# An eight-chunk tail of a recurrence moved from three steps of a software pipeline into eight

## The chip, the cores and the metric

The kernel runs on one core of one Trainium2 chip. The metric is the time of one execution on the device in microseconds. A core has a matrix engine (TensorE, PE in the profile), a vector engine (VectorE, DVE), a scalar engine (ScalarE, ACT), GpSimd (POOL) and a queue that issues transfers (SyncE, SP). Each engine runs its own instructions strictly in the order in which they are written, and the engines wait for each other by semaphores. PE's clock is granted at one of two levels, 1.2 or 2.4 GHz; the profile gives it as a share of the higher.

## What is computed

An input x of 2048 tokens by 128 features goes through two residual blocks. The first is a linear layer trained while it runs: a scan over all tokens, each of which changes the matrix W. The second is six layers of windowed attention and a gated feed-forward part over the same tokens.

```python
def step(W, inp):
    xt, vt = inp
    y = xt @ W.T
    err = y - vt
    gW = scale * (err.T @ xt)
    return (W - eta * gW, y)
_, ys = jax.lax.scan(step, W0, (xs, vs))
...
for i in range(DEPTH):
    x = attn_layer(shift_tokens(x), Wqkv[i], q_scale[i], k_scale[i], Wo[i]) + x
    x = ffn_layer(shift_tokens(x), ln_g[i], ln_b[i], W1[i], b1[i], W2[i], b2[i]) + x
...
x = x + _layernorm(_L0_attn_ref(_layernorm(x, axis=-1), ...), axis=-1)
x = x + _layernorm(_L0_ffn_ref(_layernorm(x, axis=-1), ...), axis=-1)
```

## The kernel before

**Tiles and chunks.** The 2048 tokens are 16 tiles of 128. For the scan the same 128 tokens are called a chunk. The part of the scan inside each chunk is solved for all chunks ahead of time (up to about 57 us). What is left is a chain over the chunks, since W passes from one to the next. Chunk c takes four instructions, each of which waits for the one before: PE's `chain_w` (L436, a product with W), VectorE's `chain_u` (L745, subtracts), PE's `chain_d` (L444, the update's product) and VectorE's `chain_W` (L751, adds it to W, `wT`). `chain_w` of the next chunk needs the new W.

**Units.** The results of the chunks go on in groups, `UNITS` = tiles (0,1), (2,3), (4 to 7), (8 to 11), (12 to 15). For unit u: `result(u)` on VectorE (an addition L760 with two inputs in SBUF, statistics L764 and L769); `layer_norm(u, 0)` on GpSimd (four small instructions, L1283 to L1289), then on ScalarE (L1023); `total(u)` on VectorE (the residual, L777 to L785); `layer_norm(u, 1)` on GpSimd and ScalarE; `features(u)` on PE (L453, a transpose into a bank of PSUM) and `featured(u)` on ScalarE (L1032, L1033), which fills x0S, the input of the main stage. Tile t can be projected when its unit's features are there.

**The main stage.** It begins at about 77 us and is a software pipeline written out by hand: every engine runs a loop over s, and in turn s it does the first part of tile s, the second of tile s-1 and so on down to tile s-5 (96 pairs of layer and tile, then the feed-forward parts in groups of four tiles). Per tile, PE projects keys and queries into psq (L257), in two halves of 16 products; VectorE reads each half twice (L947 and L961 for the first, L825 and L841 for the second) before ScalarE squares it (L1124, L1200), and only then may PE write the next half. GpSimd adds and scales (L1332, L1391, L1352, L1368), PE transposes the result into two of four ring banks (L267), scores it (L298), and VectorE takes the maximum (L983), subtracts (L816), sums (L857), GpSimd normalises (L1373), VectorE transposes (L978) and PE mixes (L309) with the values (L279). VectorE's L947 for tile t waits for the projection of tile t and for the transposes of tile t-2. The ring of four PSUM banks is handed out in the order of PE's program by `take`; a product waits until its bank's former contents are copied out. The chain and the features take banks from the same ring.

**Where the chain sits.** Chunks 0 to 3 and units 0 and 1's results run ahead of the loop. The others have slots inside the turns: `chunk_at(s, j)` says which chunk has slot j of turn s, and `unit_at(s, lag)` which unit has a slot in turn s. Slots 0 and 1 are in turn s (slot 0 before L947 of tile s, slot 1 after it), slots 2 and 3 stand in turn s+1. In GpSimd's loop `layer_norm(u, 0)` stands between L1352 and L1368, and `layer_norm(u, 1)` ahead of L1346. SP loads the second layer's projection matrix into `wqk[:, 1]`, which holds `c_xn`, an operand of `chain_d`, until the last chunk is through.

Of the kernel before, what the change touches and what calls it, by code (L numbers as in the profile page):

```python
# [16 lines left out]
QUAD = 4  # L17
GROUPS = TILES // QUAD
# [19 lines left out]
UNITS = [(0, 2), (2, 2), (4, 4), (8, 4), (12, 4)]  # L38
# [9 lines left out]
def group_at(s, lag):  # L48

    n = s - lag  # L50
    return n // QUAD if n >= 0 and n % QUAD == 0 and n // QUAD < ALLG else -1


def chunk_at(s, j):

    return QUAD * (s + 1) + j if 0 <= s < GROUPS - 1 else -1


def unit_at(s, lag):

    u = s - lag + 2
    return u if 1 <= u < len(UNITS) else -1


def build(nc, x_d, wvT_d, w0T_d, bv_d, eta_d, wqk_d, scale_d, mvT_d, wo_d, w1_d, w2_d, par_d,
          ident_d, rep_d, mask_d, rope_d, kfac_d, level_d, out_d):
    ctx = ExitStack()
    with ctx:
# [157 lines left out]
        def wait(eng, s, value):  # L226

            if isinstance(value, int) and value <= 0:
                return
            eng.wait_ge(s, value)  # L230
# [15 lines left out]
        def _(pe):  # L246
# [261 lines left out]
            for s in range(STEPS + 20):  # L508
                if chunk_at(s - 1, 1) >= 0:
                    chain_w(chunk_at(s - 1, 1))  # L510
# [15 lines left out]
                if chunk_at(s - 1, 1) >= 0:  # L526
                    chain_d(chunk_at(s - 1, 1))
# [49 lines left out]
                if chunk_at(s - 1, 3) >= 0:  # L577
                    chain_w(chunk_at(s - 1, 3))
                u = unit_at(s, 3)
                if u >= 0:  # L580
                    features(u)
# [100 lines left out]
        def _(dve):  # L682
# [123 lines left out]

            for s in range(STEPS + 20):
                u = unit_at(s, 2)
                if u >= 0:
                    total(u)  # L810
# [89 lines left out]
                if i >= 0:  # L900
# [5 lines left out]
                    v.scalar_tensor_tensor(uT[0:rows, 2, :], ring[bank][0:rows, :], par[0:rows, i // GROUPS, 4:5],  # L906
                                           uT[0:rows, 2, :], ALU.add, ALU.mult).then_inc(freed[bank], 1)
                u = unit_at(s, 1)
                if u >= 2:
                    result(u)  # L910
# [483 lines left out]
        @block.sync  # L1394
        def _(sp):
            x_v = x_d.rearrange("(t p) d -> p t d", p=P)

            def load_x(g):
                sp.dma_start(xmid[:, QUAD * g:QUAD * g + QUAD, :], x_v[:, QUAD * g:QUAD * g + QUAD, :]).then_inc(a_x[g], 16)

            load_x(0)
            sp.dma_start(ident[:, :], ident_d).then_inc(s_ident, 16)
            load_x(1)
            sp.dma_start(eta_bc[:, :], eta_d.partition_broadcast(P)).then_inc(s_level, 16)
            load_x(2)
            sp.dma_start(level, level_d).then_inc(s_level, 16)
            load_x(3)
            for dst, src in ((wvT, wvT_d), (wT[:, :], w0T_d), (bv, bv_d.partition_broadcast(P))):
                sp.dma_start(dst, src).then_inc(s_const, 16)
            for dst, src in ((kfac[:, :], kfac_d), (mask_in, mask_d), (rope[:, :, :], rope_d), (rep_in, rep_d),  # L1410
                             (qk_scales[:, :, :], scale_d.partition_broadcast(P)), (par[:, :, :], par_d)):
                sp.dma_start(dst, src).then_inc(s_tables, 16)
            sp.dma_start(wqk[:, 0, :], wqk_d[0]).then_inc(wqk_ready, 16)

            def load_m(l):
                sp.dma_start(mvT[:, :, :], mvT_d[l]).then_inc(mw_ready, 16)
                sp.dma_start(wo[:, :, :], wo_d[l].rearrange("(a p) n -> p a n", p=P)).then_inc(mw_ready, 16)

            def load_w1(l):
                sp.dma_start(w1[:, :], w1_d[l]).then_inc(w1_ready, 16)  # L1420

            def load_w2(l):
                sp.dma_start(w2[:, 0:2, :], w2_d[l, 0:256, :].rearrange("(a p) n -> p a n", p=P)).then_inc(w2_ready, 16)
                sp.dma_start(w2[0:HID + 1 - 256, 2, :], w2_d[l, 256:HID + 1, :]).then_inc(w2_ready, 16)

            load_m(0)
            load_w1(0)
            load_w2(0)
            bank, n = place["H3", 0]
            sp.wait_ge(filled[bank], n + 1)  # L1430
            load_m(1)
            out_v = out_d.rearrange("(t p) d -> p t d", p=P)

            for s in range(STEPS + 20):
                i = group_at(s, 8)
                if i >= 0:
                    g = i % GROUPS
                    bank, n = place["Y", QUAD * i + QUAD - 1]
                    sp.wait_ge(freed[bank], n + 1)
                    wait(sp, xh_ready, i)  # L1440
                    tiles = slice(1 + QUAD * g, 1 + QUAD * g + QUAD)
                    sp.dma_start(xf[:, 0], x1[:, 0, tiles, :]).then_inc(xf_ready, 16)
                    sp.dma_start(xf[1:P, 1], x1[0:P - 1, 1, tiles, :]).then_inc(xf_ready, 16)
                    sp.dma_start(xf[0:1, 1], x1[P - 1:P, 1, QUAD * g:QUAD * g + QUAD, :]).then_inc(xf_ready, 16)
                l = s // TILES
                if s == GROUPS:
                    bank, n = place["cd", TILES - 1]
                    sp.wait_ge(filled[bank], n + 1)
                    sp.dma_start(wqk[:, 1, :], wqk_d[1]).then_inc(wqk_ready, 16)
                if s % TILES == 0 and 1 <= l < LAYERS - 1:  # L1450
                    sp.wait_ge(pq_done, TILES * l)
                    sp.dma_start(wqk[:, (l + 1) % 2, :], wqk_d[l + 1]).then_inc(wqk_ready, 16)
                if s % TILES == LOAD_M and l < LAYERS - 2:
                    bank, n = place["H3", l + 1]
                    sp.wait_ge(filled[bank], n + 1)
                    load_m(l + 2)
                if s % TILES == LOAD_W and 1 <= l < LAYERS:
                    bank, n = place["A2", GROUPS * l - 1]
                    sp.wait_ge(filled[bank], n + 1)
                    load_w1(l)  # L1460
                    bank, n = place["Z", GROUPS * l - 1]
                    sp.wait_ge(filled[bank], n + 1)
                    load_w2(l)
                i = group_at(s, 18)
                if i >= LASTG:
                    g = i - LASTG
                    sp.wait_ge(f_out, g + 1)
                    sp.dma_start(out_v[:, QUAD * g:QUAD * g + QUAD, :], xmid[:, QUAD * g:QUAD * g + QUAD, :]).then_inc(s_out, 16)

            sp.wait_ge(s_out, 16 * GROUPS)  # L1470
# [81 lines left out]
```

## Time and profile before

| | us |
|---|---|
| median of 3 runs | 1506.65 (1505.9 to 1509.11) |
| profiled execution | 1507.59 |
| its span, first to last instruction | 1505.8 |
| PE busy | 1441.7 |
| VectorE busy | 1327.1 |
| GpSimd busy | 1209.8 |
| ScalarE busy | 1162.2 |

The span is cut below into steps: a step runs from VectorE's start of L947 for one tile to its start for the next. Step 0 begins at 81.6 us. In the rows of the timeline the columns are start, length (both us), engine, line, operation, output and input, count, and in brackets the idle time just before it and what ended it.

### The profile page before, as it was taken

To read this page: it belongs to the slowest core of one execution; us is meant where nothing else is said; L and a number is where in the kernel's file an instruction comes from. 1 tells how busy PE (TensorE), PEld (TensorE's weight loads), DVE (VectorE), ACT (ScalarE), POOL (GpSimd) and SP (SyncE) were. 2 spreads that over 40 slices of the span, in tenths; PEclk is the share of its full clock that TensorE was granted. 3 is DMA by queue.
4 is the path that set the end of the run, shared out by engine and by line. 5 is a ranking of instruction groups with operands and counts; after the bars stand their busy time and mean duration, and the time that the engine had idled before them with its cause. 6 is when DMAs were issued, how large, how long until landed. Compare 5 with 4: busy or idle time off the path is not lost.

```text
span 1505.8 us, 74802 instructions
## 1 busy us (share of the span) xinstructions
PE 1441.7 (96%) x32904; PEld 785.9 (52%) x32904; DVE 1327.1 (88%) x1789; ACT 1162.2 (77%) x2289; POOL 1209.8 (80%) x1051
## 2 busy tenths in 40 slices
PE   6877999999999999999999999999999999999985
PEld 6823444545545545545545545545555545545553
DVE  5478999989999989999999999989999999999974
ACT  4337888878888788888888888888888788888871
POOL 5148999878888888888888888888888888888841
PEclk9968999999999999999999999999999999999998
DMA  5100000020000020000020000020000000000000
GB/s 206 30 1 30 3 10 10 3 66 10 4 20 15 4 66 10 3 20 15 3 66 10 4 19 15 4 66 10 3 20 15 4 10 10 4 20 15 4 17 29
DMA packets 24564, 32.93 MB, mean 22 GB/s; under 512 B 2372, under 2 KB 21424, under 8 KB 23344
## 3 DMA queue, kind: packets, MB, share of 16 engines
q1 hardware_dynamic: 24240, 28.15, 5.8%
q8 instruction: 260, 4.26, 1.2%
q14 instruction: 64, 0.52, 0.1%
HBM read 20.80 MB, written 1.05 MB: 15 GB/s over the span
## 4 chain that ended last, share of the span: by engine, by line
PE 89%; DVE 5%; issue 2%; POOL 2%; ACT 1%; DMA 1%; SPq 0%; POOLq 0%; DVEq 0%; ACTq 0%
PE psq L257 22%; PE ring L279 21%; PE ring L309 11%; PE pss L298 9%; PE ring L267 9%; PE ring L323 8%; PE ring L333 4%; PE ring L346 1%; DVE qa L825 1%; PE ring L382 1%; DVE qb L841 1%; DVE mx L983 1%; DVE qb L961 1%; DMA xf<-x 0%; DMA mh<-in_bv 0%
## 5 line engine op out<-in xcount | busy, mean ns | idle before, releaser
L279 PE MATMUL ring<-mh,x0S 128*32 128x512 f32 x3072 | 407.9, 595 | 0.0
L257 PE MATMUL psq<-wqk,x0S 128*32 128x512 f32 x3072 | 394.9, 612 | 5.9 <-ACT sq L1200 4.9
L1332 POOL TENSOR_TENSOR qa<-qa,qb 128x1024 f32<-128x1024 f32 x96 | 229.2, 2388 | 6.7 <-DVE qb L961 6.7
L1391 POOL TENSOR_TENSOR qa<-qa,qb 128x1024 f32<-128x1024 f32 x96 | 228.6, 2382 | 0.0
L309 PEld LDWEIGHTS ring<-u,pT 128*32 128x32 f32 x6144 | 171.4, 111 | 61.8 <-issue 60.1
L309 PE MATMUL ring<-u,pT 128*32 128x128 f32 x6144 | 191.6, 274 | 4.1 <-DVE pT L978 4.1
L1373 POOL TENSOR_TENSOR pr<-pr,rden 128x1024 f32<-128x1024 f32 x96 | 183.9, 1916 | 12.8 <-DVE rden L860 12.8
L257 PEld LDWEIGHTS psq<-wqk,x0S 128*32 128x32 f32 x3072 | 93.6, 111 | 184.2 <-issue 168.4
L1352 POOL TENSOR_TENSOR qa<-qa,rn 128x1024 f32<-128x1024 f32 x96 | 182.7, 1903 | 0.2
L1368 POOL TENSOR_TENSOR qa<-qa,rn 128x1024 f32<-128x1024 f32 x96 | 182.8, 1904 | 0.0
L298 PEld LDWEIGHTS pss<-kT,qT 64*32 64x32 f32 x12288 | 134.8, 105 | 91.1 <-issue 83.6
L947 DVE TENSOR_TENSOR qa<-psq,tab 128x1024 f32<-128x1024 f32 x96 | 117.5, 1224 | 71.3 <-PE ring L267 71.0
L298 PE MATMUL pss<-kT,qT 64*32 64x64 f32 x12288 | 166.6, 224 | 2.6 <-issue 2.4
L279 PEld LDWEIGHTS ring<-mh,x0S 128*32 128x32 f32 x3072 | 95.5, 109 | 134.0 <-issue 120.8
L267 PEld LDWEIGHTS ring<-ident,qa 64*128 64x128 f32 x3072 | 111.5, 139 | 78.1 <-issue 50.7
L1346 POOL TENSOR_TENSOR tab<-rope,qk_scales 128x256 f32<-128x256 f32 x96 | 70.6, 736 | 101.2 <-DVE qb L841 101.2
L323 PE MATMUL ring<-xh,w 128*32 128x512 f32 (+1 forms) x1056 | 148.2, 594 | 1.2 <-ACT xh L1170 1.2
L1200 ACT ACTIVATE sq<-psq 128x1024 f32<-128x1024 f32 x96 | 98.2, 1023 | 60.0 <-DVE qb L841 58.6
L267 PE MATMUL ring<-ident,qa 64*128 64x64 f32 x3072 | 136.6, 229 | 5.2 <-issue 3.0
L825 DVE TENSOR_TENSOR qa<-psq,tab 128x1024 f32<-128x1024 f32 x96 | 116.9, 1218 | 9.4 <-PE psq L257 8.5
L983 DVE TENSOR_REDUCE mx<-pss 128x16 f32<-128x1024 f32 x96 | 114.8, 1196 | 10.4 <-PE pss L298 10.4
L978 DVE STREAM_TRANSPOSE pT<-pr 128x1024 f32<-128x1024 f32 x96 | 118.7, 1237 | 2.9 <-POOL pr L1373 2.7
(172 smaller groups left out, 2724.3 us busy)
## 6 DMA issues: line engine op xcount, KB each, us to landing
wqk<-in_wqk SPq DMA_DIRECT2D x6, 1024.0 KB, 8.6
mvT<-in_mvT SPq DMA_DIRECT2D x6, 512.0 KB, 3.8
wo<-in_wo SPq DMA_DIRECT2D x6, 512.0 KB, 5.2
xf<-x SPq DMA_DIRECT2D x24, 128.0 KB
xf<-x SPq DMA_DIRECT2D x24, 127.0 KB
rope<-in_rope SPq DMA_DIRECT2D x1, 2048.0 KB, 10.0
w<-in_w SPq DMA_DIRECT2D x6, 341.0 KB, 3.0
xmid<-in_x SPq DMA_DIRECT2D x4, 256.0 KB, 4.2
```

The costliest lines, as they stand in the source:

```text
L257: last = mm(psq[WIN * w:WIN * w + WIN, 512 * (n % 2):512 * (n % 2) + 512], x0S[:, tile * P + WIN * w:tile * P + WIN * w + WIN], wqk[:, l % ...
L267: last = tr(banks[r][:, 64 * blk:64 * blk + 64], src(blk)[rows], ident[rows, rows])
L279: last = mm(bank[WIN * g:WIN * g + WIN, :], x0S[:, tile * P + WIN * w:tile * P + WIN * w + WIN], mh[:, l % 2, g, :, :].rearrange("p j n -> ...
L298: last = mm(pss[WIN * g:WIN * g + WIN, col:col + KEYS], qT[rows, pair, WIN * w:WIN * w + WIN], kT[rows, t % 2, pair, WIN * w:WIN * w + KEY ...
L309: last = mm(bank[WIN * w:WIN * w + WIN, 0:P], pT[:, half, b * P + WIN * w:b * P + WIN * w + WIN], u4[:, slot, v_w, b * P:b * P + P], start ...
L323: last = mm(bank[c:c + m, :], w1[:, col + c:col + c + m], xnT[:, :], start=True, stop=True)
L825: v.tensor_tensor(a3[t % 2][:, 0:16, :], q3, tab[:, t % 2, 0, :].unsqueeze(1).broadcast_to([P, HEADS, HD]), ALU.mult)
L1332: g_.tensor_tensor(qa[:, t % 2, 1024:2048], qa[:, t % 2, 1024:2048], qb[:, 1024:2048], ALU.add).then_inc(sum_k, 1)
L1352: g_.tensor_tensor(a3[t % 2][:, 16:32, :], a3[t % 2][:, 16:32, :], rn[:, 16:32].unsqueeze(2).broadcast_to([P, HEADS, HD]), ALU.mult).then_ ...
L1368: g_.tensor_tensor(a3[t % 2][:, 0:16, :], a3[t % 2][:, 0:16, :], rn[:, 0:16].unsqueeze(2).broadcast_to([P, HEADS, HD]), ALU.mult).then_inc ...
L1373: g_.tensor_tensor(p4[t % 2], p4[t % 2], rden[:, :].unsqueeze(1).unsqueeze(3).broadcast_to([P, 2, HEADS, WIN]), ALU.mult).then_inc(p_ready, 1)
L1391: g_.tensor_tensor(qa[:, t % 2, 0:1024], qa[:, t % 2, 0:1024], qb[:, 0:1024], ALU.add).then_inc(sum_q, 1)
```

## The change

In three steps of the loop four chunks each are replaced by a table. Chunks 4 to 7 and unit 1 and 2 keep their slots. Chunk 8 moves from slot 0 of turn 1 to slot 1 of turn 1; chunks 9 to 15 have slot 0 of turns 2 to 8, one each. Unit 3's slots move from those of s - lag = 1 to s - lag = 4, and unit 4's from 2 to 8. The load of the second layer's projection matrix moves from turn 4 to turn 8, since it must follow chunk 15.

```diff
--- before.py
+++ after.py
@@ -51,15 +51,19 @@
     return n // QUAD if n >= 0 and n % QUAD == 0 and n // QUAD < ALLG else -1
 
 
+CHUNKS = {(0, 0): 4, (0, 1): 5, (0, 2): 6, (0, 3): 7, (1, 1): 8, (2, 0): 9, (3, 0): 10, (4, 0): 11,
+          (5, 0): 12, (6, 0): 13, (7, 0): 14, (8, 0): 15}
+UNIT_STEP = {-1: 1, 0: 2, 4: 3, 8: 4}
+
+
 def chunk_at(s, j):
 
-    return QUAD * (s + 1) + j if 0 <= s < GROUPS - 1 else -1
+    return CHUNKS.get((s, j), -1)
 
 
 def unit_at(s, lag):
 
-    u = s - lag + 2
-    return u if 1 <= u < len(UNITS) else -1
+    return UNIT_STEP.get(s - lag, -1)
@@ -1443,7 +1447,7 @@
                 l = s // TILES
-                if s == GROUPS:
+                if s == 2 * GROUPS:
                     bank, n = place["cd", TILES - 1]
                     sp.wait_ge(filled[bank], n + 1)
                     sp.dma_start(wqk[:, 1, :], wqk_d[1]).then_inc(wqk_ready, 16)
```

Counted in steps as cut above, the chunks whose four instructions fall into each are, before: 5 to 8 in step 0, 9 to 12 in step 1, 13 to 15 in step 2; after: 5 to 7, then 8 and 9, and one in each of steps 2 to 7 (10 to 15). On VectorE result(3) moves from step 1 to step 4, total(3) from 2 to 5, result(4) from 2 to 8, total(4) from 3 to 9.

## Rows read from the trace of the kernel before

**Rows 1.** Page, part 1: busy us, share of span, instructions.

```profile
PE 1441.7 (96%) x32904; PEld 785.9 (52%) x32904; DVE 1327.1 (88%) x1789; ACT 1162.2 (77%) x2289; POOL 1209.8 (80%) x1051
```

**Rows 2.** Steps 0 to 11: stretch, length, busy by engine, PEclk, DMA share, GB/s.

```profile
81.60:98.00 16.40, 11.54 (x48) 4.39 (x48) 13.88 (x29) 4.20 (x8) 7.49 (x11) 0.69 0.00 1
98.00:115.40 17.40, 12.92 (x68) 5.42 (x68) 13.74 (x34) 6.23 (x17) 10.94 (x16) 0.71 0.00 0
115.40:130.60 15.20, 12.39 (x172) 5.69 (x175) 13.20 (x32) 11.08 (x27) 11.20 (x14) 0.89 0.20 70
130.60:146.60 16.00, 11.23 (x189) 4.14 (x190) 13.96 (x22) 12.19 (x26) 15.51 (x17) 0.89 0.01 3
146.60:159.40 12.80, 12.51 (x317) 6.51 (x295) 12.10 (x14) 11.12 (x24) 10.71 (x10) 1.00 0.01 3
159.40:171.50 12.10, 11.97 (x319) 6.08 (x296) 12.00 (x14) 9.61 (x20) 10.97 (x10) 1.00 0.01 3
171.50:183.90 12.40, 12.19 (x316) 6.13 (x294) 12.10 (x14) 9.69 (x20) 11.73 (x10) 1.00 0.02 5
183.90:196.80 12.90, 12.90 (x323) 6.96 (x308) 12.06 (x13) 10.50 (x22) 12.22 (x10) 1.00 0.06 16
196.80:209.60 12.80, 12.65 (x356) 6.66 (x343) 12.69 (x17) 10.26 (x21) 11.77 (x10) 1.00 0.04 11
209.60:222.40 12.80, 11.58 (x256) 5.61 (x257) 12.27 (x19) 9.69 (x21) 12.48 (x14) 1.00 0.01 3
222.40:235.00 12.60, 12.00 (x320) 6.11 (x298) 12.14 (x14) 10.37 (x22) 11.91 (x10) 1.00 0.01 3
235.00:247.40 12.40, 12.40 (x316) 6.30 (x298) 12.05 (x13) 10.48 (x22) 11.71 (x10) 1.00 0.06 17
```

**Rows 3.** Timeline of VectorE: the end of step 0, chunks 8 and 9.

```profile
97.75 0.35 DVE L751 SCALAR_TENSOR_TENSOR wT<-ring,coef,wT 128x128 f32<-128x128 f32 x1 [1.86 <-PE ring L444]
98.02 1.22 DVE L947 TENSOR_TENSOR qa<-psq,tab 128x1024 f32<-128x1024 f32 x1
99.15 0.28 DVE L745 TENSOR_TENSOR x0S<-ring,x0S 128x128 f32<-128x128 f32 x1
```

**Rows 4.** Timeline of PE: projections in steps 0, 3 and 6.

```profile
93.34 3.64 PE L257 MATMUL psq<-wqk,x0S 128*32 128x512 f32 x16
...
142.21 3.54 PE L257 MATMUL psq<-wqk,x0S 128*32 128x512 f32 x16 [3.64 <-ACT sq L1200]
...
181.13 1.92 PE L257 MATMUL psq<-wqk,x0S 128*32 128x512 f32 x16
```

**Rows 5.** Page, part 5: busy us, mean ns of one, idle time before.

```profile
L1200 ACT ACTIVATE sq<-psq 128x1024 f32<-128x1024 f32 x96 | 98.2, 1023 | 60.0 <-DVE qb L841 58.6
```

**Rows 6.** Timeline of VectorE: result(2) with its successor, total(4) with its successor.

```profile
92.58 0.69 DVE L760 TENSOR_TENSOR x0T<-x0T,x0S 128x512 f32<-128x512 f32 x1
...
94.50 0.26 DVE L745 TENSOR_TENSOR x0S<-ring,x0S 128x128 f32<-128x128 f32 x1
...
134.11 2.20 DVE L777 TENSOR_TENSOR xmid<-xmid,x0T 128x512 f32<-128x512 f32 x1
...
137.55 1.19 DVE L816 TENSOR_TENSOR pr<-pss,mx 128x1024 f32<-128x1024 f32 x1
```

**Rows 7.** Timeline of GpSimd around layer_norm(4, 0).

```profile
125.79 1.91 POOL L1352 TENSOR_TENSOR qa<-qa,rn 128x1024 f32<-128x1024 f32 x1
129.65 0.20 POOL L1283 TENSOR_TENSOR lvare<-lmv,eps 128x4 f32<-128x4 f32 x1 [1.95 <-DVE lmv L769]
...
131.52 1.90 POOL L1368 TENSOR_TENSOR qa<-qa,rn 128x1024 f32<-128x1024 f32 x1
```

**Rows 8.** Timeline of VectorE: L978 in step 6.

```profile
174.14 1.25 DVE L978 STREAM_TRANSPOSE pT<-pr 128x1024 f32<-128x1024 f32 x1 [0.19 <-POOL pr L1373]
```

**Rows 9.** Timeline of PE: the transposes at the end of step 4.

```profile
158.51 0.71 PE L267 MATMUL ring<-ident,qa 64*128 64x64 f32 x16 [0.29 <-ACT x0S L1033]
```

**Rows 10.** Timeline of PE: a stall in the second layer.

```profile
309.33 0.97 PE L298 MATMUL pss<-kT,qT 64*32 64x64 f32 x48 [2.37 <-issue]
```

## The prediction, made before the changed kernel was run

> **What bounds the kernel now.** I read the table of engine shares first, then the main stage's opening cut into steps, then single rows of the timeline. Over the whole span PE is busy 96%, and a reader could stop there [rows 1]. The change touches only the first twelve steps of the main stage, and there the table by step says something else [rows 2]. I cut it where VectorE starts L947 for the next tile, so that one row is one step and a delay anywhere ends up in some row's length. Steps 0 to 3 last 16.4, 17.4, 15.2 and 16.0 us at a mean granted clock of 0.69 to 0.89, and no engine is full: this is latency. From step 4 a step takes 12.1 to 12.9 us, and in it VectorE is busy 12.0 to 12.7, PE 11.6 to 12.9 and GpSimd 10.7 to 12.5. So the change moves work from steps in which engines wait for each other into steps in which three engines are nearly full. After step 11 PE is full and later steps only carry the shift on. The question is thus what L947 of tile 12 (now at 247.4) does.
>
> **What the first steps give back.** Up to chunk 7 nothing moves. In step 0 VectorE waits 1.86 us for chunk 8's second product before it can start L947 [rows 3]; in the new order chunk 8 comes after L947, so tile 1 starts at about 95.8, just after the projection that began at 92.1 instead of 93.3 [rows 4]. That is -2.2 us. What then limits a step is the loop through psq: project, two VectorE passes, a square of 1.02 [rows 5], and the same again. A projection costs 3.64 at the low clock and 1.92 at the high one [rows 4]. Step 1 has two at the low clock: 2 x 3.6 + 4 x 1.2 + 2 x 1.0, and 2.7 for the features of tiles 2 and 3, chunk 9 and the transpose that the loop also passes, is 16.7. Step 1 loses result(3) and two of its four chunks, step 2 loses total(3), result(4) and two of three chunks, step 3 loses total(4) and gets chunk 11; I walked steps 2 and 3 in the same way as step 1. Step 2 has its second projection at the high clock, because PE then works without a gap for some six microseconds: 13.4. In step 3, total(4) no longer keeps VectorE from releasing psq (it holds it from 134.11 to 137.55 [rows 6]), PE's idle 3.64 before a 3.54 projection [rows 4] shrinks to about 1.1, and the projection costs 1.92: 12.0. Steps 0 to 3 become 14.2, 16.7, 13.4 and 12.0 against 16.4, 17.4, 15.2 and 16.0: **-8.7**. If PE stays at the low clock in both disputed projections the gain is 3.3 less, -5.4; if it were high in all the others too, three more projections give 1.65 each, -13.7.
>
> **What the later steps pay.** Four things arrive in steps 4 to 9. (a) One chunk a step in 4 to 7. On VectorE L745 and L751 have 0.28 and 0.35 [rows 3], of which overlap leaves about 0.2 and 0.27 (97.75 to 98.02): 0.47 a step in a step that has 0.1 to 0.8 idle. On PE a chunk adds two products, some 0.85; that binds only in step 7, where PE is busy 12.90 of 12.90 and VectorE has room [rows 2]. (b) result(u) in steps 4 and 8: 92.58 to 94.50, 1.92, if GpSimd leaves it alone; total(u) in steps 5 and 9 costs about 2.0 likewise, but 3.44 where its first instruction met a running GpSimd one, 2.20 instead of 0.69 [rows 6]. (c) GpSimd's layer_norm(u, 0) stands in its queue ahead of L1368 and L1373. Now it waits 1.95 for result(4)'s statistics, and L1368 starts at 131.52, 3.8 after L1352 ended at 127.70 [rows 7]. There nobody needed GpSimd. In a full step VectorE's L978 has already waited 0.19 for L1373 [rows 8], so a delay of 3.8, less what result(u) itself adds on VectorE, goes through to L978: about 1.8. (d) While VectorE does all this PE has nothing: I get gaps of 3.5 and 5.7 us before the projections for tiles 6 and 10, like the 3.64 that preceded a low-clock projection, so 1.65 more each.
>
> Step 4: 12.12 of VectorE work + 0.47 + 1.92 = 14.5 (from 12.8, **+1.7**). PE's second product of chunk 12 waits there for a chain_u that is queued behind result(3), some 1.6 us, and the transposes of tile 3 behind it; they end as VectorE gets there, so this costs nothing beyond the 14.5. Step 5: 12.1 + 0.47 + 2.0 + 1.8 + 1.9 (projection and chain at the low clock) = 18.3 (from 12.1, **+6.2**). Step 6: 12.1 + 0.47 + 0.7 for featured(3), which frees a ring bank that the transpose wants (a wait for it of 0.29 stands in step 4 now [rows 9]) = 13.3 (from 12.4, **+0.9**). Step 7: 12.9 + 0.85 = 13.8 (**+0.9**). Step 8: 12.8 + 1.92 = 14.7 (**+1.9**). Step 9: 12.8 + 2.0 for L978 + 3.55 for total(4), which meets L1391 here because GpSimd has the feed-forward part's first statistics in that step too (12.48 of 12.80 [rows 2]), + 1.6 for the clock, less 0.4 of idle = 19.6 (**+6.8**). Step 10: +0.3 for featured(4). Together **+18.7**.
>
> The 1 MB load of wqk[1] moves on SP from step 4 to step 8, behind the xf loads. Tile 16 needs it eight steps, some 100 us, later: nothing waits for it.
>
> **Sum.** -8.7 + 18.7 = +10.0. The profiled execution took 1507.59 (span 1505.8), the median is 1506.65, 0.9 lower; on the median this gives 1516.6, and I say **1516.5**, slower by 0.66%.
>
> A rule of the Trainium skill stands beside (b): the page GPSIMD Engine Reference, section Specifications, says that GpSimd shares its SBUF interfaces with VectorE and that the conflict is with VectorE instructions that have two SBUF inputs. The 2.20 against 0.69 is what that looks like. I take the long form for one of the four moved instructions; by the rule alone, with GpSimd busy nearly all the time, all four would pay it, about 4 us more.
>
> **The rivals.** *Hidden in the slack.* VectorE is idle 0.1 to 0.8 in each of steps 4 to 11, 3.4 in all [rows 2]. The moved VectorE work is 4 x 0.47 + 2 x 1.92 + 2 x 2.0 = 9.7. If GpSimd's queue and the clock cost nothing, the later steps pay between 9.7 - 3.4 = 6.3 and 9.7, and the whole is -2.4 to +1.0: 1504 to 1508. For it: GpSimd too is idle 0.3 to 2.1 in each of these rows. Against it: L978 already waits for L1373. The Trainium skill, Perfetto Trace Analysis, section Optimization Strategy, says that interleaving regimes with different bounds may help; by it the time would come out at this rival's.
>
> *Faster.* With VectorE and PE no longer waiting for the chain, the clock rises in step 1 rather than step 2, and all projections of steps 1 and 2 cost 1.92. The gain is then 13.7, and if the later steps pay only the 9.7 less 3.4 the time is 1506.65 - 7.4 = 1499. It decides if PE's gaps ahead of those projections nearly vanish; I count 2 to 3 us in each, since both VectorE passes and the square lie between two projections, so it is unlikely.
>
> *A late clock.* PE has fewer products in steps 2 and 3 than now, and the clock stays low to tile 4: gain 5.4, time 1520.
>
> *The load in a worse place.* PE once stood 2.37 us with no releaser [rows 10] right as SP issued xf loads and a wqk load. The new step 8 puts these two together: +2.4 if it recurs, 1519. Now only one of the later loads shows as much.
>
> *Nothing moves*, because the chain's waits are replaced one for one by others: covered by the first rival's 1507.
>
> **How the numbers follow.** Forecast 0.50; hidden in the slack 0.18, of which 0.03 below 1503.6; faster 0.07; late clock 0.15; the load 0.10. The measurement can tell about 0.2%, 3 us, from no change. So faster 0.10, same 0.15, slower 0.75. The range takes in the two slower rivals and half of the slack rival: 1505 to 1520.5. It leaves out the faster case and all collisions at once.
>
> **What would show it.** L947 by tile, shift against now: -2.2, -2.9, -4.7, -8.7 for tiles 1 to 4, then -7.0, -0.8, 0, +1, +3, +10, +10 up to tile 11. L978 waiting 1.5 to 2 us for L1373 in steps 5 and 9; GpSimd waiting about 2 us or more for L769 twice among full steps; 3.5 us projections for tiles 6 and 10. I am wrong if tile 4 is not at least 5 us earlier, or if steps 5 and 9 stay under 15 us.

## The result, and the profile of the changed kernel

| | before | changed |
|---|---|---|
| median of 5 runs each | 1505.9 | 1518.14 |
| lowest to highest | 1501.76 to 1509.11 | 1515.67 to 1520.56 |
| profiled execution, its span | 1507.59, 1505.8 | 1518.14, 1516.1 |

The ratio is 1.0085, 95% interval 1.0061 to 1.011: the change makes the kernel slower by 0.85%. The changed kernel was timed once more, beside the last experiments, with 1.0058 (1.004 to 1.0075). The time is in the forecast range; the forecast point was 1516.5.

In the listings of the changed kernel every line from the loops on has a number 4 higher: L951 is the L947 of before, L982 the L978, L261 the L257. The first view is the page's part 1, which answers to [rows 1].

```profile
PE 1443.2 (95%) x32904; PEld 786.7 (52%) x32904; DVE 1326.0 (87%) x1789; ACT 1162.1 (77%) x2289; POOL 1210.3 (80%) x1051
```

Nothing is to be seen there: the same instructions, all engines busy as long as before to 1.5 us, and the span 10.3 us longer. The next view cuts the same stretch as [rows 2] at VectorE's starts of L951, one row for each of steps 0 to 11 (stretch, length, busy by engine, PEclk, DMA share, GB/s).

```profile
81.60:96.30 14.70, 11.39 (x45) 3.88 (x45) 13.37 (x27) 2.81 (x4) 5.39 (x8) 0.58 0.00 1
96.30:112.60 16.30, 10.91 (x65) 4.05 (x67) 10.08 (x20) 7.58 (x20) 14.04 (x16) 0.65 0.00 0
112.60:126.50 13.90, 10.87 (x96) 3.86 (x100) 7.73 (x9) 7.68 (x18) 7.59 (x8) 0.75 0.01 2
126.50:138.70 12.20, 10.50 (x260) 4.97 (x245) 11.34 (x14) 8.90 (x19) 9.91 (x9) 1.00 0.01 1
138.70:153.60 14.90, 12.97 (x313) 6.67 (x298) 14.41 (x24) 9.60 (x20) 11.30 (x12) 1.00 0.02 4
153.60:169.90 16.30, 12.89 (x321) 6.69 (x308) 14.44 (x25) 11.89 (x26) 15.69 (x16) 1.00 0.01 2
169.90:183.40 13.50, 13.50 (x329) 7.07 (x308) 12.70 (x17) 11.42 (x24) 12.67 (x11) 1.00 0.01 2
183.40:198.80 15.40, 14.12 (x336) 7.73 (x313) 12.76 (x16) 10.75 (x22) 13.43 (x11) 1.00 0.07 20
198.80:213.40 14.60, 14.43 (x376) 7.11 (x360) 14.46 (x26) 11.06 (x22) 8.38 (x9) 1.00 0.23 77
213.40:233.50 20.10, 13.32 (x226) 5.83 (x231) 15.85 (x27) 12.23 (x28) 19.37 (x22) 0.76 0.01 2
233.50:246.50 13.00, 12.79 (x324) 6.80 (x309) 12.24 (x14) 11.00 (x24) 10.34 (x10) 0.98 0.01 3
246.50:258.80 12.30, 12.30 (x327) 6.43 (x305) 11.99 (x14) 10.51 (x22) 11.19 (x10) 1.00 0.06 17
```

Steps 0 to 3 are 7.8 us shorter than before, steps 4 to 11 are 19.2 longer, and steps 5 and 9 hold 11.5 of that. Their sum is +11.4 while the span is 10.3 longer, so 1.1 us is given back after step 11; what lies there is told of below the table of steps. What ended the waits in the two long steps is in the timeline. The next rows are VectorE's, in steps 5, 7 and 9; the last of them begins step 10.

```profile
157.88 1.25 DVE L982 STREAM_TRANSPOSE pT<-pr 128x1024 f32<-128x1024 f32 x1 [1.75 <-POOL pr L1377]
160.16 0.80 DVE L781 TENSOR_TENSOR xmid<-xmid,x0T 128x512 f32<-128x512 f32 x1
197.99 0.35 DVE L755 SCALAR_TENSOR_TENSOR wT<-ring,coef,wT 128x128 f32<-128x128 f32 x1 [2.10 <-PE ring L448]
218.15 1.25 DVE L982 STREAM_TRANSPOSE pT<-pr 128x1024 f32<-128x1024 f32 x1 [2.00 <-POOL pr L1377]
220.43 2.43 DVE L781 TENSOR_TENSOR xmid<-xmid,x0T 128x512 f32<-128x512 f32 x1
233.52 1.22 DVE L951 TENSOR_TENSOR qa<-psq,tab 128x1024 f32<-128x1024 f32 x1 [2.16 <-PE ring L271]
```

The two L982 rows answer to [rows 8], where the wait was 0.19: VectorE now waits 1.75 and 2.00 us for GpSimd's normalisation L1377. Why that is late is in GpSimd's rows, which answer to [rows 7].

```profile
152.19 0.20 POOL L1287 TENSOR_TENSOR lvare<-lmv,eps 128x4 f32<-128x4 f32 x1 [1.95 <-DVE lmv L773]
154.07 1.90 POOL L1372 TENSOR_TENSOR qa<-qa,rn 128x1024 f32<-128x1024 f32 x1
...
212.47 0.20 POOL L1287 TENSOR_TENSOR lvare<-lmv,eps 128x4 f32<-128x4 f32 x1 [2.71 <-DVE lmv L773]
214.34 1.90 POOL L1372 TENSOR_TENSOR qa<-qa,rn 128x1024 f32<-128x1024 f32 x1
```

GpSimd stands 1.95 and 2.71 us in layer_norm(u, 0), waiting for result(u)'s statistics, and the tile's own work (L1372, L1377) waits in its queue behind it. PE's projections, which answer to [rows 4], complete the picture.

```profile
123.36 1.92 PE L261 MATMUL psq<-wqk,x0S 128*32 128x512 f32 x16
...
166.76 1.92 PE L261 MATMUL psq<-wqk,x0S 128*32 128x512 f32 x16 [2.54 <-ACT sq L1204]
...
194.51 1.16 PE L350 MATMUL ring<-wo,mvT 64*128 64x128 f32 x16 [1.17 <-ACT u L1217]
...
217.13 3.56 PE L261 MATMUL psq<-wqk,x0S 128*32 128x512 f32 x16
...
228.66 3.64 PE L261 MATMUL psq<-wqk,x0S 128*32 128x512 f32 x16 [4.50 <-ACT sq L1204]
```

In step 9 PE is idle 4.50 us and then projects at the low clock, 3.64 us instead of 1.92, as it did after 3.64 idle us before [rows 4]; the first projection of that step, 3.56, is at the low clock too. In step 5 the gap is 2.54 and the projection in this execution stayed at 1.92.

### The profile page after: what moved, and what is told of

Its sections match the earlier page's. It is cut to its first block, busy times and chain, and to the rows that moved or that the text cites. A ratio compares the mean times of both kernels' runs of the same rounds, so it can differ in the third digit from the quotient of the medians.

```text
span 1516.1 us, 74802 instructions
## 1 busy us (share of the span) xinstructions
PE 1443.2 (95%) x32904; PEld 786.7 (52%) x32904; DVE 1326.0 (87%) x1789; ACT 1162.1 (77%) x2289; POOL 1210.3 (80%) x1051
## 4 chain that ended last, share of the span: by engine, by line
PE 90%; DVE 5%; issue 2%; ACT 2%; POOL 1%; DMA 1%; SPq 0%; POOLq 0%; DVEq 0%; ACTq 0%
PE psq L261 23%; PE ring L283 21%; PE ring L313 11%; PE pss L302 10%; PE ring L271 9%; PE ring L327 8%; PE ring L337 4%; PE ring L350 1%; PE ring L386 1%; DVE qa L829 1%; DVE qb L845 1%; DMA xf<-x 0%; DVE qb L965 0%; ACT sq L1204 0%; ACT wqk L1000 0%
## 5 line engine op out<-in xcount | busy, mean ns | idle before, releaser
L261 PE MATMUL psq<-wqk,x0S 128*32 128x512 f32 x3072 | 397.5, 615 | 17.8 <-ACT sq L1204 8.5
L1395 POOL TENSOR_TENSOR qa<-qa,qb 128x1024 f32<-128x1024 f32 x96 | 228.5, 2381 | 0.0
L1377 POOL TENSOR_TENSOR pr<-pr,rden 128x1024 f32<-128x1024 f32 x96 | 183.8, 1914 | 12.8 <-DVE rden L864 12.8
L261 PEld LDWEIGHTS psq<-wqk,x0S 128*32 128x32 f32 x3072 | 94.0, 111 | 191.9 <-issue 163.1
L1356 POOL TENSOR_TENSOR qa<-qa,rn 128x1024 f32<-128x1024 f32 x96 | 182.6, 1902 | 0.2
L1372 POOL TENSOR_TENSOR qa<-qa,rn 128x1024 f32<-128x1024 f32 x96 | 182.7, 1903 | 0.0
L951 DVE TENSOR_TENSOR qa<-psq,tab 128x1024 f32<-128x1024 f32 x96 | 117.5, 1224 | 71.9 <-PE ring L271 71.8
L987 DVE TENSOR_REDUCE mx<-pss 128x16 f32<-128x1024 f32 x96 | 114.9, 1197 | 10.3 <-PE pss L302 10.3
L982 DVE STREAM_TRANSPOSE pT<-pr 128x1024 f32<-128x1024 f32 x96 | 118.7, 1236 | 5.7 <-POOL pr L1377 5.6
```

The lines of the kernel that those rows point to most:

```text
L261: last = mm(psq[WIN * w:WIN * w + WIN, 512 * (n % 2):512 * (n % 2) + 512], x0S[:, tile * P + WIN * w:tile * P + WIN * w + WIN], wqk[:, l % ...
L1356: g_.tensor_tensor(a3[t % 2][:, 16:32, :], a3[t % 2][:, 16:32, :], rn[:, 16:32].unsqueeze(2).broadcast_to([P, HEADS, HD]), ALU.mult).then_ ...
L1372: g_.tensor_tensor(a3[t % 2][:, 0:16, :], a3[t % 2][:, 0:16, :], rn[:, 0:16].unsqueeze(2).broadcast_to([P, HEADS, HD]), ALU.mult).then_inc ...
L1377: g_.tensor_tensor(p4[t % 2], p4[t % 2], rden[:, :].unsqueeze(1).unsqueeze(3).broadcast_to([P, 2, HEADS, WIN]), ALU.mult).then_inc(p_ready, 1)
L1395: g_.tensor_tensor(qa[:, t % 2, 0:1024], qa[:, t % 2, 0:1024], qb[:, 0:1024], ALU.add).then_inc(sum_q, 1)
```

## The experiments

The theory from the prediction: it is not the chain but what was moved with it, the units' work, that costs the time, by three mechanisms: GpSimd's place in its queue, VectorE's own added work, and PE's low clock after the gaps these make. The rivals: the chunks themselves cost it, or the low clock alone. All step lengths below are differences of VectorE's starts of L951 (or its equivalent), for steps 0 to 11, with their sum, from one profiled execution of each kernel. The last column is what follows, from VectorE's start for tile 12 to the end of the span:

```
before          16.4 17.4 15.2 16.0 12.8 12.1 12.4 13.0 12.8 12.8 12.6 12.5  165.8  1258.4
changed         14.8 16.3 13.9 12.2 15.0 16.3 13.5 15.4 14.7 20.1 12.9 12.3  177.2  1257.3
changed again   14.8 16.3 13.9 12.2 14.4 17.8 13.5 15.1 14.7 20.1 12.8 12.3  177.7  1256.7
GpSimd order    14.8 15.7 14.0 12.2 14.4 14.5 13.7 15.1 15.8 14.9 13.9 12.3  171.2  1259.8
chunk 15        14.8 16.3 13.8 12.2 14.6 17.6 13.5 13.8 14.7 20.1 13.1 12.3  176.8  1257.6
units only      15.8 17.4 14.3 11.8 14.1 18.0 12.8 13.0 14.7 20.1 12.9 12.3  177.1  1256.6
busy PE         14.8 15.6 14.0 12.2 14.7 17.7 13.5 15.4 14.7 18.0 13.9 12.3  176.8  1254.6
thin units      14.8 16.3 13.9 12.2 13.8 16.6 13.7 15.1 14.6 14.8 13.6 12.3  171.7  1259.8
three a step    14.8 16.4 14.7 16.5 17.0 12.9 12.2 13.0 12.8 12.8 12.6 12.5  168.1  1257.2
 + GpSimd order 14.8 15.9 14.8 15.5 16.4 12.9 12.2 13.0 12.8 12.8 12.6 12.5  166.0  1255.0
one late unit   16.8 16.1 14.8 14.0 18.5 13.1 12.1 13.0 12.8 12.8 12.6 12.5  168.8  1259.2
before + GpSimd 16.4 17.4 15.2 13.4 12.9 12.1 12.4 13.0 12.8 12.8 12.6 12.5  163.3  1254.1
 + five rounds  16.6 17.3 14.9 13.4 12.9 12.1 12.4 13.0 12.8 12.8 12.6 12.5  163.2  1256.8
 + features     15.8 17.4 15.2 13.0 13.1 12.1 12.4 13.0 12.8 12.8 12.6 12.5  162.5  1254.4
```

The rows "before + GpSimd" and "+ five rounds" are one kernel, taken twice; the last row also moves the features' copy.

The last column moves by 5.7 us, and not with the schedules: the kernel taken twice has 1254.1 and 1256.8. Much of it is one stall. In nine of the fourteen executions PE stands 1.55 to 2.37 us in the second layer with no releaser, as in [rows 10], and the eight steps from tile 12 on take 115.1 to 116.3 us; in the other five (busy PE, both with three a step, the first of the kernel taken twice, features) there is no such stall and they take 112.3 to 112.8. The changed kernel has it too:

```profile
320.14 0.72 PE L302 MATMUL pss<-kT,qT 64*32 64x64 f32 x48 [1.83 <-issue]
```

What brings it on no run shows. With it the times of single executions differ by some 3 us whatever the schedule is, so the experiments with one run are read by their steps.

**GpSimd's place alone.** The changed kernel with layer_norm(u, 0) behind the normalisation in GpSimd's loop:

```diff
-                u = unit_at(s, 2)
-                if u >= 0:
-                    layer_norm(u, 0)
                 t = s - 3
...
                                      ALU.mult).then_inc(p_ready, 1)
+                u = unit_at(s, 2)
+                if u >= 0:
+                    layer_norm(u, 0)
                 i = group_at(s, 10)
```

> The changed kernel with one edit: in GpSimd's loop layer_norm(u, 0) stands behind the normalisation (L1377 there) instead of ahead of L1372. If the queue order is what makes VectorE's transpose L982 wait (1.75 us in step 5, 2.00 in step 9), both waits go, step 5 falls from 16.3 to about 14.6, step 9 from 20.1 to about 18.1, tile 12 starts 3.7 us earlier and the time is about 1514.5. The rival, that GpSimd is simply overfull and the delay moves on to its next additions, gives steps 5 and 9 the same length as now and a time of 1518.

Measured: 1514.65, ratio 1.0042 (1.0026 to 1.0059). Both waits of L982 are gone, steps 5 and 9 lose 1.8 and 5.2 us, and the sum 6.0. VectorE's rows in steps 8 and 9:

```profile
207.36 1.77 DVE L764 TENSOR_TENSOR x0T<-x0T,x0S 128x512 f32<-128x512 f32 x1
...
214.12 1.23 DVE L982 STREAM_TRANSPOSE pT<-pr 128x1024 f32<-128x1024 f32 x1
...
216.39 1.45 DVE L781 TENSOR_TENSOR xmid<-xmid,x0T 128x512 f32<-128x512 f32 x1
```

Step 9 loses more than L982's 2.0: L781 takes 1.45 instead of 2.43, and PE's gap ahead of the second projection is 1.16 instead of 4.50 and the projection takes 1.92. Steps 8 and 10 give 1.1 and 1.0 back; in step 8 it is L764, 1.77 instead of 0.67, since GpSimd no longer waits but works beside it. Step 1 is 0.6 shorter as well, but there PE's first projection happened to take 3.09 us instead of 3.64, and the edit doesn't reach it: busy PE has 15.6 there without the edit, thin units 16.3 with it. In the device times less is to be seen: 1514.65 beside 1515.41 for the changed kernel again, with intervals that overlap, while the result's own interval (1.0061 to 1.011) lies above this one. The largest single cost that was found in the steps is thus where four small instructions stand in one queue.

**Chunk 15 in its neighbour's slot.** The changed kernel with chunk 15 in slot 1 of turn 7, a slot earlier in program order:

```diff
-          (5, 0): 12, (6, 0): 13, (7, 0): 14, (8, 0): 15}
+          (5, 0): 12, (6, 0): 13, (7, 0): 14, (7, 1): 15}
```

> The changed kernel with chunk 15 in slot 1 of turn 7 instead of slot 0 of turn 8, so that turn 8's merge products take ring banks without the chain ahead of them. If the 1.17 us wait of the merge for a copy of values (step 7, 194.51) comes from the two banks that the chain takes there, step 7 falls from 15.4 to about 13.8 and tile 12 starts 1.6 us earlier. The rival, that the merge pays for its place and not for the banks, leaves step 7 at 15.4.

Measured: 1516.8 in one run; step 7 falls from 15.39 to 13.82, which is the 13.8 that had been forecast for it. The wait of L350 for a ring bank (1.17 above) is gone: chunk 15's product had taken the bank ahead of it. In the second execution of the changed kernel, told of below, step 7 is 15.1 and the clock in step 5 the same as here; against that one tile 12 starts 0.9 us earlier and not 1.6, since steps 4 and 10 are 0.2 and 0.3 longer. The same execution settles something else. Its step 5 is 17.64, not 16.27, and PE's row there is

```profile
165.29 3.30 PE L260 MATMUL psq<-wqk,x0S 128*32 128x512 f32 x16 [2.54 <-ACT sq L1203]
```

The gap is the same 2.54 us, and this time the projection is at the low clock.

**The units alone.** The chunks back in turns 0 to 2 as before, the units and the load as in the changed kernel:

```diff
+CHUNKS = {(0, 0): 4, (0, 1): 5, (0, 2): 6, (0, 3): 7, (1, 0): 8, (1, 1): 9,
+          (1, 2): 10, (1, 3): 11, (2, 0): 12, (2, 1): 13, (2, 2): 14, (2, 3): 15}
+UNIT_STEP = {-1: 1, 0: 2, 4: 3, 8: 4}
```

> The chunks where the kernel before has them (four a step in three steps), the units where the changed kernel has them (units 3 and 4 in turns 5 to 8 and 9 to 12). If the units are what costs, steps 4 to 9 lose only the chain's 0.5 us each: tile 4 starts about 5.5 us earlier than before, tile 12 about 9 us later than before, and the time is about 1514. The rival, that the chain's instructions in full steps are what costs, has tile 12 about 4 us earlier than before and a time of about 1502.

Measured: 1517.78, ratio 1.0073 (1.005 to 1.0095), which lies between the changed kernel's two ratios, and the same sum, 177.1. Steps 8 and 9 are the same to 0.01. Tile 4 starts 5.6 us earlier than before, as expected, and tile 12 starts 11.3 later instead of 9, with the low clock in step 5. Spreading the chain saves 2.2 us in steps 0 to 3 (59.3 to 57.1) and costs 2.2 in steps 4 to 7 (57.8 to 60.1; with the second execution of the changed kernel, told of below, 2.9): nothing, or a loss of 0.7. Moving the units saves 5.6 in steps 0 to 3 and costs 16.9 later. The rival by which the chunks cost the time is out.

**PE kept busy through the gap.** The changed kernel, with PE's second product of values done five more times in turn 10:

```diff
+                    if s == 10:
+                        for _ in range(5):
+                            values(ring[bank], t, 1)
                     values(ring[bank], t, 1).then_inc(filled[bank], 1)
```

> The changed kernel; in turn 10 PE repeats the second product of values five times into the same bank before it signals it, 4.3 us of work in the gap of 4.5 us ahead of the projection of tile 10 (228.66). If the low clock after that gap is part of the price, the projection costs 1.9 us instead of 3.64, step 9 falls from 20.1 to about 18.4 and tile 12 starts 1.7 us earlier. The rival, that something else ends at the same time (GpSimd's L1356 at 230.3), leaves at most 0.5 us of it.

Measured: 1513.23 in one run; step 9 falls by 2.10 and step 10 rises by 0.95. PE's projection in step 9:

```profile
227.81 1.92 PE L261 MATMUL psq<-wqk,x0S 128*32 128x512 f32 x16 [1.22 <-ACT sq L1207]
```

The gap ahead of it is 1.22 instead of 4.50 and it is at the high clock: the low clock is a real term of step 9, some 2 us, but a net 1.15, since a step that comes early meets other waits (0.43 for kT, 0.60 for a square in step 10). It is not the whole. The first projection of step 9 tells something too. It came ahead of the edit and was at the high clock in this execution, 1.92 instead of 3.56, yet the second one began 15.28 us after the step's start, and 15.25 in the changed kernel. VectorE came for the first one's result much later, so its clock cost nothing. The time of 1513.23 is lower than the steps explain, because the stall in the second layer is absent.

**VectorE's part made thin.** As the first experiment, and for units 3 and 4 VectorE's additions and statistics on one tile instead of four; the other three tiles' work is left out:

```diff
+                if u >= 3:
+                    size = 1
                 rows = x0T[:, t0:t0 + size, :]
...
+                if u >= 3:
+                    size = 1
                 rows = xmid[:, t0:t0 + size, :]
```

> The new order, with GpSimd's layer_norm(u, 0) moved behind its normalisation as in the earlier experiment, and for the units u of 3 and above VectorE's part of result(u) and total(u) (the addition and the statistics) on one of the four tiles instead of four; three quarters of that VectorE work are left out, while GpSimd's and ScalarE's part stays. Theory, the moved VectorE work is what steps 4, 5, 8 and 9 pay: they fall from 14.41, 14.47, 15.75 and 14.91 by 1.5 to 3 us each, to about 12.6 to 13.3, the steps from tile 0 to tile 12 add up to about 163 to 165, and the time is 1504 to 1507. Rival, the length comes from what is queued on the other engines (GpSimd's normalisation, ScalarE's features) or from the chunks: the four steps stay above 14, the sum stays at 171 and the time at 1513 to 1515.

Measured: 1514.0 in one run, and a sum of 171.7 instead of 171.2. The theory fell in this form: only steps 4 and 8 answered (14.41 to 13.80, 15.75 to 14.60), step 9 by 0.1, and step 5 became longer, 14.47 to 16.64. Two groups of rows say why. First VectorE's additions in steps 8 and 9, with the statistics behind the first, and the GpSimd instruction that runs when each begins:

```profile
208.69 1.38 DVE L766 TENSOR_TENSOR x0T<-x0T,x0S 128x128 f32<-128x128 f32 x1
210.10 0.29 DVE L770 BATCH_NORM_STATS2 lbst<-x0T 128x6 f32<-128x128 f32 x1
...
216.56 1.49 DVE L785 TENSOR_TENSOR xmid<-xmid,x0T 128x128 f32<-128x128 f32 x1
```

```profile
208.00 1.91 POOL L1373 TENSOR_TENSOR qa<-qa,rn 128x1024 f32<-128x1024 f32 x1
...
215.55 2.35 POOL L1399 TENSOR_TENSOR qa<-qa,qb 128x1024 f32<-128x1024 f32 x1
```

A quarter of the addition takes 1.38 and 1.49 us beside a running GpSimd instruction; in step 4, where it began in the last 0.15 us of one, it took 0.28. Both long ones end 0.15 to 0.16 us after GpSimd's instruction ends. In the first experiment, with four tiles, they took 1.77 and 1.45 and ended 0.55 and 0.54 after it. What shrinks with the size is this last part; the wait for the rest of GpSimd's instruction does not. Second, ScalarE in step 5, where it stands with layer_norm(u, 0) ahead of the square of tile 5:

```profile
155.03 1.65 ACT L1031 ACTIVATE x0T<-x0T,lnmr,lrstd 128x128 f32<-128x128 f32 x4 [1.18 <-POOL lnmr L1297]
156.59 1.00 ACT L1132 ACTIVATE sq<-psq 128x1024 f32<-128x1024 f32 x1
```

The same square in the first experiment:

```profile
156.60 1.00 ACT L1128 ACTIVATE sq<-psq 128x1024 f32<-128x1024 f32 x1
```

VectorE began step 5 0.79 us earlier and was done with its second pass at 153.94, but the square started at the same time to 0.01: it is queued behind ScalarE's layer_norm(u, 0), 1.65 us, and that waits for GpSimd. PE's gap before the projection grew by what VectorE had saved, from 1.39 to 2.15, and the projection was at the low clock:

```profile
157.64 3.20 PE L261 MATMUL psq<-wqk,x0S 128*32 128x512 f32 x16 [2.15 <-ACT sq L1132]
```

Of the 2.17 us by which step 5 is longer than in the first experiment, 0.79 is the earlier start against a square that did not move, and 1.28 the clock of this projection. So the unit's work on GpSimd and ScalarE is a cost of its own beside VectorE's, which shows once VectorE's part is shrunk. In the changed kernel itself the square of step 5 starts at 157.36, 1.36 after VectorE's second pass ends at 156.00, and it costs nothing there: the projection behind it ends at 160.34, and VectorE comes for its result at 163.30; in step 9 it is not late (216.05 after 216.02), since VectorE comes late too. A version with ScalarE's part behind the square was not run.

**The changed kernel again**, beside the thin kernel and the last two below:

> The changed kernel once more, on the same chip as the runs beside it. Both theories: ratio 1.006 to 1.011 to the kernel before. What it tells apart: if the 2.54 us gap of PE ahead of the projection in step 5 always leads to a 1.92 us projection in this kernel, step 5 is again 16.3 us; if the level of the clock after such a gap varies from execution to execution, step 5 is 17.6 to 18.0 with a projection of about 3.3 in this profile.

Measured: 1515.41, ratio 1.0058 (1.004 to 1.0075), step 5 now 17.76, and PE's row in it:

```profile
165.13 3.43 PE L261 MATMUL psq<-wqk,x0S 128*32 128x512 f32 x16 [2.52 <-ACT sq L1204]
```

So the same kernel after the same gap has either clock. Of the five profiled executions with the units' new places and GpSimd's old order (two of the changed kernel, chunk 15, units only, busy PE) four were at the low clock there, with step 5 from 17.6 to 18.0; the profile of the result is the exception.

**Other spreads.** Two ways to take less out of the first steps: three chunks a step with both units inside the first five steps, without and with GpSimd's new order, and one that moves only unit 4, by one turn, with chunks 12 to 14 each a slot later and chunk 15 in slot 1 of turn 3. In all three the load of the projection matrix moves to turn 5.

```diff
+CHUNKS = {(0, 0): 4, (0, 1): 5, (0, 2): 6, (0, 3): 7, (1, 1): 8, (1, 2): 9, (1, 3): 10,
+          (2, 1): 11, (2, 2): 12, (2, 3): 13, (3, 1): 14, (3, 2): 15}
+UNIT_STEP = {-1: 1, 0: 2, 2: 3, 3: 4}
```

> Three chunks a step and none in slot 0, ahead of which VectorE waits for PE: chunks 8 to 10 in slots 1 to 3 of turn 1, 11 to 13 in those of turn 2, 14 and 15 in slots 1 and 2 of turn 3; unit 3 from turn 3 on, unit 4 from turn 4 on; SP's load in turn 5. If what counts is that the units' work falls into steps in which VectorE and GpSimd have room, this lies between the two kernels: steps 0 to 2 near the changed kernel's, result(3) and result(4) in steps 2 and 3, total(4) alone in step 4, tile 12 at 1 us before to 4 us after its place in the kernel before, time 1505 to 1510. The rival, that the number of chunks in full steps counts, has it at the kernel before's gain of steps 0 to 2 in full, 1498 to 1502.

> The same schedule with GpSimd's layer_norm(u, 0) behind the normalisation. If the queue order costs only where steps are full, it gains about 2 us over the same schedule without it, in steps 3 and 4. The rival, that it costs nothing so early, leaves them equal.

```diff
+CHUNKS = {(0, 0): 4, (0, 1): 5, (0, 2): 6, (0, 3): 7, (1, 0): 8, (1, 1): 9,
+          (1, 2): 10, (1, 3): 11, (2, 1): 12, (2, 2): 13, (2, 3): 14, (3, 1): 15}
+UNIT_STEP = {-1: 1, 0: 2, 1: 3, 3: 4}
```

> Chunks 4 to 11 and unit 3 as in the kernel before, chunks 12 to 14 in slots 1 to 3 of turn 2, 15 in slot 1 of turn 3, unit 4 from turn 4 on. If slot 0 is what makes step 1 long (VectorE's and PE's instructions behind it wait for the projection), step 1 falls by 0.8 and step 2 by 1.5, and total(4) costs 2 to 4 in step 4 instead of in step 3, in all within 2 us of the kernel before: 1504 to 1508. The rival, that one late unit costs as much as each does in the changed kernel (some 8 us), gives 1510 or more.

Measured, one run each beside 1505.04 for the kernel before: 1508.49, 1504.79 and 1511.17; the sums are 2.3, 0.2 and 3.0 over before's. Three a step lies between the two kernels, as its theory had it, and GpSimd's order takes 2.1 out of it, 1.6 of that in steps 3 and 4. Moving unit 4 by one step costs more than it saves: steps 0 to 3 give back 3.3 and the later ones take 6.3, of which step 4 has 5.7 where 2 to 4 were expected. Its time is in the rival's range, but the rival's 8 us are not in the steps. VectorE's row in step 4 of that kernel shows the same wait again:

```profile
147.45 1.25 DVE L981 STREAM_TRANSPOSE pT<-pr 128x1024 f32<-128x1024 f32 x1 [2.27 <-POOL pr L1376]
```

**GpSimd's order in the kernel before.** The lesson of the first experiment applied to the old schedule, the same diff:

> The schedule of the kernel before, with GpSimd's layer_norm(u, 0) behind the normalisation. If GpSimd's queue order costs nothing while steps 1 to 3 have room, the time and every step stay within 0.5 us of the kernel before's. The rival, that the kernel before pays for it too (GpSimd's wait of 1.95 us at 129.65 stands ahead of L1368), has step 3 shorter by 1 to 2 us.

Measured: 1500.61 beside 1505.04. One step changes, step 3, from 15.97 to 13.44. That is 2.5 of the 4.4; this execution is also one without the stall in the second layer. The rows of VectorE and PE there answer to [rows 6] and [rows 4]:

```profile
133.77 0.68 DVE L780 TENSOR_TENSOR xmid<-xmid,x0T 128x512 f32<-128x512 f32 x1
```

```profile
140.35 1.92 PE L260 MATMUL psq<-wqk,x0S 128*32 128x512 f32 x16 [1.80 <-ACT sq L1203]
```

L780 meets only the last 0.09 us of GpSimd's instruction (0.68 for 2.20), PE's gap is 1.80 instead of 3.64, and the projection stays at the high clock (1.92 for 3.54). It was then timed in five rounds, beside a version that also copies out a unit's features ahead of the U0 copy on ScalarE:

> The schedule of the kernel before with GpSimd's layer_norm(u, 0) behind its normalisation, timed. Theory, step 3 alone shortens from 16.0 to 13.4 us and nothing gives it back: about 2.5 us less, ratio 0.998 (0.997 to 0.999). Rival, the shorter step is repaid at the next stage's start, and the single lower time came from another execution's preamble: ratio 0.9995 to 1.0005.

```diff
+                u = unit_at(s, 2)
+                if u >= 0:
+                    featured(u)
                 t = s - 2
...
-                u = unit_at(s, 2)
-                if u >= 0:
-                    featured(u)
```

> As the run beside it, and in every turn ScalarE's featured(u) ahead of the copy of U0, so that the ring bank that featured(u) reads comes free earlier. Theory, the transposes of the next steps wait for that bank: up to 0.5 us less for each of the four units, at most 1.5 us less than the run beside it. Rival, U0's copy is late by the same amount and is waited for just as much: no difference, or up to 1 us more.

Measured: 1502.08, ratio 0.9975 (0.9961 to 0.9989), and 1504.29, ratio 0.9985 (0.9973 to 0.9997). GpSimd's order makes the kernel before faster by 0.25%, about the 2.5 us of step 3. For the features' place nothing is settled: the two intervals overlap, steps 3 and 4 together are 26.1 instead of 26.3, and the medians point the other way. The theory's saving is not borne out by the times.

## Why the prediction was right, and which of its terms were off

**What bounds, and the direction.** Steps 0 to 3 were latency and gave back 7.8 us (forecast 8.7); from step 4 on the engines were full and took 19.2 (forecast 18.7). On the medians of the result that is 12.2 us against a forecast of 10.0. That the sum of the later steps agrees so well is partly luck: step 5 came out 2.0 shorter than forecast by its clock, step 7 1.6 longer by a term left out, and in the changed kernel's second execution the later steps took 19.8.

**The first steps.** 14.8, 16.3, 13.9 and 12.2, forecast 14.2, 16.7, 13.4 and 12.0. Step 2's second projection (123.36 above) and all of step 3 are at the high clock, as said; PE had no gap from 116.12 on. The term that was off most is step 0's, 0.6: tile 1's projection began at 92.64 and not at 92.1, as the one before it took 3.64 where it had taken 3.00 in the kernel before. Tile 4 came 7.9 earlier, forecast 8.7. Most of this is the units' and not the chain's: with the units moved alone tile 4 already gains 5.6 of it.

**GpSimd's queue (c).** The term was 1.8 in step 5 and 2.0 in step 9; L982 waited 1.75 and 2.00. The mechanism was right, and it was worth more than its wait: reordering took 7.0 us out of steps 5 and 9 and 6.0 out of the twelve, not 3.7. In step 9 L982's 2.00, an L781 shorter by 1.0 and a projection shorter by 1.7 make 4.7 of the 5.2. The prediction counted these as separate terms; in the steps they went together.

**The chunks (a).** 0.47 in VectorE-bound steps and 0.85 in step 7. Step 6 is 12.80 without its chunk and 13.45 with it, 0.65. Step 7 was missed, 15.39 for 13.8: the term left out that chunk 15's product takes the ring bank that L350 of the same step wants. With it moved the step is 13.82.

**result and total (b).** Steps 4 and 8 were forecast at 14.5 and 14.7 and are 15.0 (14.4 in the second execution) and 14.7. One of the four additions took the long form, L781 in step 9 with 2.43; the others took 0.69, 0.67 and 0.80. The prediction had set the Trainium skill's rule (GPSIMD Engine Reference, Specifications: shared SBUF interfaces, conflicts with VectorE instructions of two SBUF inputs) against that, by which all four would pay. The trace agrees with the rule and shows its price here. L781 in step 9 began at 220.43 beside this instruction, and ended 0.55 us after it:

```profile
219.95 2.36 POOL L1395 TENSOR_TENSOR qa<-qa,qb 128x1024 f32<-128x1024 f32 x1
```

In step 5 L781 began 0.04 us before L1395 ended, and in step 4 L764 0.15 us before L1356 did, so there was next to nothing to wait for; in step 8 GpSimd was waiting in layer_norm(u, 0) for that very result. Once it no longer waited, the same addition took 1.77. So one long form in four came true by the timing of this schedule, which the prediction had not worked out. From L781 to L820 total(4) took 3.67 us for the 3.55 of the sum.

**The clock (d).** Gaps of 3.5 and 5.7 were forecast ahead of the second projections of steps 5 and 9, with low clock after both; the gaps were 2.54 and 4.50. The low clock came in step 9 (3.64) and, in this execution, not in step 5: hence 16.3 where 18.3 was forecast. In the four other executions with the units' new places and GpSimd's old order it came, and step 5 was 17.6 to 18.0. The forecast of 18.3 is thus right in size for the usual case. Step 9 is 20.1 for 19.6; both its projections were at the low clock, and the first of them cost nothing.

**What wasn't seen.** ScalarE's layer_norm(u, 0) stands directly ahead of the square that frees psq. The prediction walked the queues of VectorE, GpSimd, PE and SP and took ScalarE's share only as featured(u). In step 5 this delays the square by 1.36 us. That cost nothing in the changed kernel, and 0.79 us with a thinner VectorE load.

**The load and the late clock.** The load of the projection matrix is issued in step 7 (197.98) beside the xf loads, and step 8 shows no stall of PE. That rival rested on the stall of [rows 10], which comes and goes between executions and which the changed kernel has as well, 1.83 us at 320.14. The eight steps around it take 116.3 us before and 115.1 in the changed kernel, which is the 1.1 given back after step 11; it says nothing about the change. The clock was not late: step 3 ran wholly at the high level. The rival hidden in the slack fell with steps 5 and 9 at 16.3 and 20.1. The Trainium skill's advice on interleaving regimes (Perfetto Trace Analysis, Optimization Strategy) had stood for it; in this kernel the two regimes were interleaved and the time rose by 0.85%, since work that the full steps needed stood in the queues behind the pieces moved in.

## What to carry to other kernels

Work that is moved off a latency-bound stretch into a full one costs more than its own time: it brings its waits with it into in-order queues, and every instruction queued behind such a wait is late. Before spreading work, list for each engine what stands right behind each moved piece, and first try to put the piece behind the work that someone is waiting for: here four small GpSimd instructions moved down by two places took 6.0 us out of the twelve steps of the new schedule (less in its device times) and made the old one 0.25% faster, with no spreading at all. A price that comes from a collision with another engine's running instruction, or from a wait for a third engine, is reduced little by making the moved work smaller. And before a difference of 2 or 3 us between single executions is put down to a change, see whether it lies in the steps that were changed.

## What the runs showed of the hardware

A gap of PE of the same length may or may not be followed by the low clock: after 2.54 us the projection took 1.92 in one execution and 3.30 in another, after 2.52 it took 3.43, after 2.15 with a thinner VectorE load 3.20; after the gaps of 1.80, 1.39 and 1.22 named above it took 1.92.

A VectorE addition with two inputs in SBUF that begins beside a running GpSimd instruction of 128x1024 ends a fixed time after that one: 0.54 to 0.56 us later for 128x512 in the 41 cases of these runs in which the two overlapped by 0.1 us or more, 0.28 or 0.29 for 128x256 (86.81 after 86.53 in step 0 of the changed kernel) and 0.14 to 0.16 for 128x128. Its price is thus the rest of GpSimd's instruction and its own part: 0.67 to 0.69 us for 128x512 alone and up to 2.43 beside GpSimd, for 128x128 0.28 beside the last 0.14 us of one and up to 1.49 otherwise.

The stall of PE in the second layer, 1.55 to 2.37 us with no releaser, was there in nine profiled executions of fourteen, and one kernel had it in one execution and not in the other.
